# Sharing the last pair's store out in seven DMAs instead of one: two per-batch 128 x 128 maps with residuals, on one core

## The chip, the cores and the metric

One core of a Trainium2 chip runs the kernel. The metric is the device time of one execution in microseconds; lower is better. The kernel before was run three times: 644.12, 644.40 and 645.06 us, median 644.4. A fourth execution was taken with the hardware profiler and took 643.72 us.

## The reference

`x` is 128 batches of a 128 x 2048 float32 matrix. Each batch `b` has two condition numbers, which pick a 128 x 128 matrix out of 16 and out of 32, and a bias row out of 32:

```python
def _L0_cond_ref(x, weights, condition):
    W = weights[condition]
    return jnp.einsum('bct,bcd->bdt', x, W)

def _L1_cond_ref(x, subjects, weights, biases):
    w = weights[subjects]
    b = biases[subjects]
    out = jnp.einsum('bct,bcd->bdt', x, w)
    return out + jnp.transpose(b, (0, 2, 1))

x = x + _L0_cond_ref(x, L0_cond_weights, itok_B_0_15)
x = x + _L1_cond_ref(x, itok_B_0_31, L1_cond_weights, L1_cond_biases)
```

In float32, 134 MB of `x` come in and 134 MB go out.

## The kernel before

**The arithmetic.** Both steps are linear in `x`, so for one batch the result is one 128 x 128 matrix times the batch, plus a bias column: the product of (first matrix + identity) and (second matrix + identity). POOL adds the identities (lines 137 and 138), TensorE multiplies the two (`combine`, line 155), ACT copies the product out of PSUM (`copy_maps`, line 243).

**The tiling.** Two batches make a pair, and 64 pairs are worked off in order. A pair is one tile of `xt`, 128 partitions by 16 KB: partitions 0 to 63 hold the even batch, 64 to 127 the odd one, and a partition holds two neighbouring rows of a batch (2 x 2048 floats), which are contiguous in memory. `xt` has 8 slots. A pair's 32 matmuls (`pair` and `term`, line 160) go in two halves of 1024 columns into `acc0` (even batch) and `acc1` (odd batch). DVE evicts `acc0` with the bias added (`even_out`, lines 222 and 224), ACT evicts `acc1` (`odd_out`, line 247), both back into the slot that the input came from.

**The order.** There is no scheduler; each engine's instructions are written out, and semaphores link them.
- SP loads the two sets of matrices and then the pairs, one DMA of 128 partitions by 16 KB each (line 111). From the ninth pair on it waits until the slot's earlier pair has been stored.
- ACT evicts, waits for DVE's half and its own (lines 260 and 261), and issues the pair's store (line 262), again one DMA of 128 partitions by 16 KB. It goes straight on to the next pair.
- After the last pair, ACT waits for the stores of all eight slots (line 264). That is the end of its program.

Before the pairs, ACT also issues three small loads (lines 235 to 237): `cond_sb`, the condition numbers on one partition (1 x 1 KB); `bias_sb`, 128 partitions by 128 B; `cond_rep`, 32 partitions by 512 B.

A DMA that SP or ACT issues is cut into packets, one for each partition here, and the packets are shared among the core's 16 DMA engines. Each engine used writes a completion of a few bytes after its data packets; the semaphore counts up to 16. In the profile q1 is SP's queue (loads) and q10 is ACT's (stores and the three small loads).

The lines at the end of the program:

```python
                act.dma_start(out_pairs[q, :, :], xt[:, q % SLOTS, :]).then_inc(stored[q % SLOTS], LOAD)
            for q in range(SLOTS):
                act.wait_ge(stored[q], LOAD * TURNS)
```

Of the kernel before, what the change touches and what calls it, by code (L numbers as in the profile page):

```python
# [5 lines left out]
def conditioned_residual_kernel(  # L6
# [16 lines left out]
    B, C, T = x.shape  # L23
# [4 lines left out]
    SLOTS = 8  # L28
    PAIRS = B // 2
    TURNS = PAIRS // SLOTS  # L30
    LOAD = 16

    x_pairs = x.rearrange("(q k) (i u) t -> q (k i) (u t)", k=2, u=2)
    out_pairs = out.rearrange("(q k) (i u) t -> q (k i) (u t)", k=2, u=2)

    ctx = ExitStack()
    with ctx:  # L39
        def sb(name, shape, dt=fp32):  # L40
            return ctx.enter_context(nc.sbuf_tensor(name, shape, dt))
# [4 lines left out]
        def sem(name):  # L46
            return ctx.enter_context(nc.semaphore(name))
# [15 lines left out]
        xt = sb("xt", [C, SLOTS, 2 * T])  # L63
# [29 lines left out]
        hi_out1 = sem("hi_out1")  # L93
        x_loaded = [sem(f"x_loaded{q}") for q in range(SLOTS)]
        stored = [sem(f"stored{q}") for q in range(SLOTS)]

        w0T_v = w0T_sb[:, :, :].rearrange("p s (i u) -> p s u i", u=2)
        w1_v = w1_sb[:, :, :].rearrange("p s (i u) -> p s u i", u=2)
# [4 lines left out]
        @block.sync  # L103
        def _(sp):
            sp.dma_start(w0T_sb[:, :, :], w0T).then_inc(w0_loaded, LOAD)
            sp.dma_start(w1_sb[:, :, :], w1).then_inc(w1_loaded, LOAD)
            for q in range(PAIRS):
                slot = q % SLOTS
                if q >= SLOTS:
                    sp.wait_ge(stored[slot], LOAD * (q // SLOTS))  # L110
                sp.dma_start(xt[:, slot, :], x_pairs[q, :, :]).then_inc(x_loaded[slot], LOAD)

        @block.gpsimd
        def _(pool):
            nc.gpsimd.memset(ident[:, :], 0.0).then_inc(zeroed, 1)  # L115
            nc.gpsimd.iota(row[:, :], [[0, B]], base=0, channel_multiplier=1).then_inc(row_ready, 1)  # L116
            pool.wait_ge(zeroed, 1)
            nc.gpsimd.affine_select(out=ident[:, :], in_=ident[:, :], compare_op=ALU.not_equal, fill=1.0, base=0,  # L118
                                    pattern=[[-1, C]], channel_multiplier=1).then_inc(ident_ready, 1)
            pool.wait_ge(ident_ready, 1)  # L120
            pool.wait_ge(cond_loaded, LOAD)
            pool.wait_ge(w0_loaded, LOAD)
            pool.wait_ge(w1_loaded, LOAD)
            GROUP = 16
            for b in range(B):
                if b % GROUP == 0:
                    _, i0 = nc.values_load_multi_w_load_instructions(  # L127
                        cond_sb[0:1, 0, b:b + GROUP], engines=[POOL], min_val=0, max_val=S0 - 1,
                        skip_runtime_bounds_check_because="conditions index the maps")
                    _, i1 = nc.values_load_multi_w_load_instructions(  # L130
                        cond_sb[0:1, 1, b:b + GROUP], engines=[POOL], min_val=0, max_val=S1 - 1,
                        skip_runtime_bounds_check_because="conditions index the maps")
                q, k = b // 2, b % 2
                if q >= 2 and k == 0:

                    pool.wait_ge(combined, q - 1)
                nc.gpsimd.tensor_tensor(map0T[:, q % 2, k, :, :], w0T_v[:, bass.ds(i0[b % GROUP], 1), :, :], ident_v, ALU.add)  # L137
                nc.gpsimd.tensor_tensor(map1[:, q % 2, k, :, :], w1_v[:, bass.ds(i1[b % GROUP], 1), :, :], ident_v,  # L138
                                        ALU.add).then_inc(maps_ready, 1)
# [93 lines left out]
        @block.scalar  # L233
        def _(act):
            act.dma_start(cond_sb[:, :, :], conds).then_inc(cond_loaded, LOAD)
            act.dma_start(bias_sb[:, :], bias1).then_inc(bias_loaded, LOAD)
            act.dma_start(cond_rep[:, :], conds[0:1, 1, :].to_broadcast([S1, B])).then_inc(rep_loaded, LOAD)
            act.wait_ge(bias_ready, 1)

            def copy_maps(q):  # L240

                act.wait_ge(combined, q + 1)
                nc.scalar.activation(both[:, q % 2, :, :], acc1[:, CB:CB + 2 * C], ACT.Identity).then_inc(both_ready, 1)  # L243

            def odd_out(q, v, a):

                return nc.scalar.activation(xt[HC:C, q % SLOTS, v * T + a:v * T + a + HALF], acc1[v * HC:(v + 1) * HC, a:a + HALF],  # L247
                                            ACT.Identity, bias=bias_of[v * HC:(v + 1) * HC, 2 * q + 1:2 * q + 2])

            copy_maps(0)  # L250
            for q in range(PAIRS):
                act.wait_ge(lo_done1, q + 1)
                odd_out(q, 0, 0)
                if q < PAIRS - 1:
                    copy_maps(q + 1)
                odd_out(q, 1, 0).then_inc(lo_out1, 1)
                act.wait_ge(hi_done1, q + 1)
                odd_out(q, 0, HALF)
                odd_out(q, 1, HALF).then_inc(hi_out1, 1)
                act.wait_ge(hi_out0, q + 1)  # L260
                act.wait_ge(hi_out1, q + 1)
                act.dma_start(out_pairs[q, :, :], xt[:, q % SLOTS, :]).then_inc(stored[q % SLOTS], LOAD)
            for q in range(SLOTS):
                act.wait_ge(stored[q], LOAD * TURNS)


# [25 lines left out]
```

## Time and profile before

| | |
|---|---|
| three runs | 644.12, 644.40, 645.06 us |
| the profiled execution | 643.72 us, its span 641.6 us |
| DMA | 271.82 MB in 18931 packets, mean 424 GB/s over the span |
| PE busy | 525.4 us (82%) |
| DVE, ACT, POOL busy | 329.2, 309.4, 124.1 us |
| first to last store issued | 30.6 to 627.1 us |

The span runs from the first to the last instruction of the profiled execution; 2.1 us of the execution's time lie outside it. Busy shares are averages over stages with different limits. The DMA share of a window is the busy time of all packets that start in it over 16 engines' time; one engine that works alone shows as 0.06. A packet counts in the window in which it starts. Landing is the time from an issue until the last engine's completion.

### The profile page before, as it was taken

The page shows a single profiled execution, that of the slowest core. Times are in us where ns is not written, and L with a number is a line of the kernel's source. Part 1 is how long each engine was busy: PE and PEld are TensorE (multiplying, and loading weights), DVE is VectorE, ACT ScalarE, POOL GpSimd, SP SyncE. Part 2 cuts the span into 40 slices and gives each one's busy share as a digit, 9 for nine tenths or more (in the row PEclk, how much of TensorE's full clock was granted, in tenths as well). Part 3 has the DMA queues.
Part 4 walks back from the last instruction along what each step waited for, and adds up shares of the span by engine and source line. Part 5 has one row for each costly group of instructions (what it writes and reads, how often), then busy time and mean ns, then how long its engine had stood idle before and what let it go on. Part 6 is the DMA issues. An engine that isn't in the chain of part 4 may idle for free.

```text
span 641.6 us, 6679 instructions
## 1 busy us (share of the span) xinstructions
PE 525.4 (82%) x2564; PEld 224.2 (35%) x2564; DVE 329.2 (51%) x259; ACT 309.4 (48%) x321; POOL 124.1 (19%) x263
## 2 busy tenths in 40 slices
PE   1899999887787787887888977889878888779880
PEld 0344443333333333333333433333333333334330
DVE  0366666455545544554546445455554545455450
ACT  0466665444544544544446445355454445454450
POOL 2222222121221221221212212122112122121000
PEclk9999999899999999999989899899999889998896
DMA  8999999999999999999999999999999999999995
GB/s 361 436 396 434 429 430 431 428 433 430 429 431 432 433 431 430 430 430 434 429 431 431 430 433 431 430 432 430 431 431 431 432 431 429 431 431 431 430 430 246
DMA packets 18931, 271.82 MB, mean 424 GB/s; under 512 B 2241, under 2 KB 2274, under 8 KB 2274
## 3 DMA queue, kind: packets, MB, share of 16 engines
q1 hardware_dynamic: 9504, 137.37, 50.3%
q10 hardware_dynamic: 9410, 134.26, 48.9%
q8 instruction: 7, 0.11, 0.1%
q14 instruction: 10, 0.08, 0.0%
HBM read 137.40 MB, written 134.22 MB: 423 GB/s over the span
## 4 chain that ended last, share of the span: by engine, by line
DMA 75%; PE 19%; DVE 3%; ACT 1%; POOLq 0%; issue 0%; DVEq 0%; POOL 0%; SPq 0%; ACTq 0%
DMA out_dram<-xt 40%; DMA xt<-in_x_dram 33%; PE acc L160 17%; PE acc L155 1%; DMA w_sb<-in_w_dram 1%; DVE xt L222 1%; DVE xt L224 1%; ACT xt L247 0%; DVEq L39 0%; ACT L243 0%; POOLq L127 0%; POOLq L130 0%; POOL map0T L137 0%; POOL map L138 0%; ACT both L243 0%
## 5 line engine op out<-in xcount | busy, mean ns | idle before, releaser
L160 PE MATMUL acc<-xt,both 64*128 64x512 f32 x2048 | 489.8, 621 | 85.2 <-DMA xt<-in_x_dram 83.2
L247 ACT ACTIVATE xt<-acc,bias_of 64x1024 f32<-64x1024 f32 x256 | 283.6, 1108 | 300.2 <-PE acc L160 297.8
L160 PEld LDWEIGHTS acc<-xt,both 64*128 64x128 f32 x2048 | 196.2, 193 | 336.7 <-issue 223.5
L222 DVE TENSOR_SCALAR xt<-acc,bias_of 64x1024 f32<-64x1024 f32 x128 | 163.3, 1276 | 282.1 <-PE acc L160 282.1
L224 DVE TENSOR_SCALAR xt<-acc,bias_of 64x1024 f32<-64x1024 f32 x128 | 165.1, 1290 | 1.9
L137 POOL TENSOR_TENSOR map0T<-w0T_sb,ident 128x128 f32<-128x128 f32 x128 | 65.6, 512 | 469.6 <-PE acc L155 457.8
L138 POOL TENSOR_TENSOR map<-w_sb,ident 128x128 f32<-128x128 f32 x128 | 65.7, 513 | 0.0
L155 PEld LDWEIGHTS acc<-map,map0T 128*64 128x64 f32 x512 | 27.4, 137 | 49.3 <-issue 48.1
L155 PE MATMUL acc<-map,map0T 128*64 128x128 f32 x512 | 43.0, 287 | 0.9 <-POOL map L138 0.9
L243 ACT ACTIVATE both<-acc 128x256 f32<-128x256 f32 x64 | 24.5, 383 | 0.8
L146 PE MATMUL acc<-ident,bias_sb 128*32 128x128 f32 x2 | 0.6, 422 | 10.7 <-DMA bias_sb<-in_bias_dram 10.7
L243 ACT ACT_TABLE_LOAD x1 | 1.3, 1283 | 16.4 <-PE acc L155 16.4
L213 DVE TENSOR_TENSOR onehot<-cond_rep,row 32x128 f32<-32x128 int32 x1 | 0.3, 280 | 12.9 <-DMA cond_rep<-in_conds_dram 12.9
L146 PEld LDWEIGHTS acc<-ident,bias_sb 128*32 128x32 f32 x2 | 0.2, 142 | 10.7 <-DMA bias_sb<-in_bias_dram 10.7
L149 PE MATMUL acc<-onehot,biasT 32*128 32x128 f32 x2 | 0.8, 480 | 2.2 <-DVE biasT L215 2.2
L149 PEld LDWEIGHTS acc<-onehot,biasT 32*128 32x128 f32 x2 | 0.5, 304 | 2.6 <-DVE onehot L213 2.6
L217 DVE COPY bias_of<-acc 128x128 f32<-128x128 f32 x1 | 0.3, 291 | 0.9 <-PE acc L149 0.9
L215 DVE COPY biasT<-acc 32x128 f32<-32x128 f32 x1 | 0.3, 279 | 0.0
L118 POOL TENSOR_SCALAR_AFFINE_SELECT ident<-ident 128x128 f32<-128x128 f32 x1 | 0.3, 282 | 0.0
L115 POOL MEMSET ident<- 128x128 f32 x1 | 0.2, 204 | 0.3 <-POOLq L281 0.3
L116 POOL IOTA row<- 32x128 int32 x1 | 0.2, 224 | 0.0
L281 POOL MEMSET const-float32-0.0<- 128x1 f32 x1 | 0.1, 98 | 0.2 <-issue 0.2
(3 smaller groups left out, 0.3 us busy)
## 6 DMA issues: line engine op xcount, KB each, us to landing
xt<-in_x_dram SPq DMA_DIRECT2D x64, 2048.0 KB, 30.7
out_dram<-xt ACTq DMA_DIRECT2D x64, 2048.0 KB, 37.2
w_sb<-in_w_dram SPq DMA_DIRECT2D x1, 2048.0 KB, 9.4
w0T_sb<-in_w0T_dram SPq DMA_DIRECT2D x1, 1024.0 KB, 4.8
cond_sb<-in_conds_dram ACTq DMA_DIRECT2D x1, 1.0 KB
bias_sb<-in_bias_dram ACTq DMA_DIRECT2D x1, 16.0 KB, 9.4
cond_rep<-in_conds_dram ACTq DMA_DIRECT2D x1, 16.0 KB, 11.1
```

The costliest lines, as they stand in the source:

```text
L118: nc.gpsimd.affine_select(out=ident[:, :], in_=ident[:, :], compare_op=ALU.not_equal, fill=1.0, base=0, pattern=[[-1, C]], channel_multipl ...
L137: nc.gpsimd.tensor_tensor(map0T[:, q % 2, k, :, :], w0T_v[:, bass.ds(i0[b % GROUP], 1), :, :], ident_v, ALU.add)
L138: nc.gpsimd.tensor_tensor(map1[:, q % 2, k, :, :], w1_v[:, bass.ds(i1[b % GROUP], 1), :, :], ident_v, ALU.add).then_inc(maps_ready, 1)
L146: nc.tensor.matmul(acc0[0:S1, 0:C], bias_sb[:, :], ident[:, :], start=True, stop=True).then_inc(turned, 1)
L149: nc.tensor.matmul(acc1[:, 0:B], biasT[:, :, :], onehot[:, :], start=True, stop=True).then_inc(picked, 1)
L155: last = nc.tensor.matmul(acc1[k * HC:(k + 1) * HC, CB + u * C:CB + (u + 1) * C], map0T[:, buf, k, u, :], map1[:, buf, k, :, :], start=Tru ...
L160: return nc.tensor.matmul(acc[:, j * CHUNK:(j + 1) * CHUNK], both[k * HC:(k + 1) * HC, buf, u, :], xt[k * HC:(k + 1) * HC, slot, u * T + j ...
L213: nc.vector.tensor_tensor(onehot[:, :], cond_rep[:, :], row[:, :], ALU.is_equal).then_inc(onehot_ready, 1)
L222: nc.vector.tensor_scalar(xt[0:HC, q % SLOTS, a:a + HALF], acc0[0:HC, a:a + HALF], bias_of[0:HC, 2 * q:2 * q + 1], None, ALU.add)
L224: return nc.vector.tensor_scalar(xt[0:HC, q % SLOTS, T + a:T + a + HALF], acc0[HC:C, a:a + HALF], bias_of[HC:C, 2 * q:2 * q + 1], None, AL ...
L243: nc.scalar.activation(both[:, q % 2, :, :], acc1[:, CB:CB + 2 * C], ACT.Identity).then_inc(both_ready, 1)
L247: return nc.scalar.activation(xt[HC:C, q % SLOTS, v * T + a:v * T + a + HALF], acc1[v * HC:(v + 1) * HC, a:a + HALF], ACT.Identity, bias=b ...
```

## The change

`EVEN` is 2304 of the 4096 floats that a partition of the tile holds (9 KB of 16 KB). For the last pair alone, ACT issues a store of columns 0 to 2303 on all 128 partitions, and then six stores of the remaining 1792 columns (7 KB), which take 28, 35, 1, 28, 35 and 1 partitions in turn. Each of the six has its own semaphore, and ACT waits for them after the waits for the slots. Nothing else differs; the other 63 stores and all loads are the same.

```diff
+    EVEN = 2304
+    TAIL = [(0, 28), (28, 63), (63, 64), (64, 92), (92, 127), (127, 128)]
...
+        tail_stored = [sem(f"tail_stored{g}") for g in range(6)]
...
                 act.wait_ge(hi_out0, q + 1)
                 act.wait_ge(hi_out1, q + 1)
-                act.dma_start(out_pairs[q, :, :], xt[:, q % SLOTS, :]).then_inc(stored[q % SLOTS], LOAD)
+                if q < PAIRS - 1:
+                    act.dma_start(out_pairs[q, :, :], xt[:, q % SLOTS, :]).then_inc(stored[q % SLOTS], LOAD)
+            act.dma_start(out_pairs[PAIRS - 1, :, 0:EVEN], xt[:, SLOTS - 1, 0:EVEN]).then_inc(stored[SLOTS - 1], LOAD)
+            for g, (lo, hi) in enumerate(TAIL):
+                act.dma_start(out_pairs[PAIRS - 1, lo:hi, EVEN:2 * T],
+                              xt[lo:hi, SLOTS - 1, EVEN:2 * T]).then_inc(tail_stored[g], LOAD)
             for q in range(SLOTS):
                 act.wait_ge(stored[q], LOAD * TURNS)
+            for g in range(6):
+                act.wait_ge(tail_stored[g], LOAD)
```

The end of ACT's program, with its issues of DMAs, before (a row is an instruction, its line, what it writes and reads, partitions x elements):

```order
L247 ACTIVATE xt<-acc,bias_of 64x1024 x3
L262 DMA out_dram<-xt 128x4096
L247 ACTIVATE xt<-acc,bias_of 64x1024 x4
L262 DMA out_dram<-xt 128x4096
L39 UNCONDITIONAL_BRANCH
```

and after the change:

```order
L251 ACTIVATE xt<-acc,bias_of 64x1024 x3
L267 DMA out_dram<-xt 128x4096
L251 ACTIVATE xt<-acc,bias_of 64x1024 x4
L268 DMA out_dram<-xt 128x2304
L270 DMA out_dram<-xt 28x1792
L270 DMA out_dram<-xt 35x1792
L270 DMA out_dram<-xt 1x1792
L270 DMA out_dram<-xt 28x1792
L270 DMA out_dram<-xt 35x1792
L270 DMA out_dram<-xt 1x1792
L42 UNCONDITIONAL_BRANCH
```

One issue has become seven, at the same place: behind the last evictions and ahead of the final waits. No instruction of another engine moved.

## Rows read from the trace of the kernel before

**Rows 1.** Page: the span, and part 2, 40 equal slices (DMA: busy tenths of 16 engines)

```profile
span 641.6 us, 6679 instructions
...
DMA  8999999999999999999999999999999999999995
GB/s 361 436 396 434 429 430 431 428 433 430 429 431 432 433 431 430 430 430 434 429 431 431 430 433 431 430 432 430 431 431 431 432 431 429 431 431 431 430 430 246
```

**Rows 2.** Page, part 4: the chain that ended last, by engine

```profile
DMA 75%; PE 19%; DVE 3%; ACT 1%; POOLq 0%; issue 0%; DVEq 0%; POOL 0%; SPq 0%; ACTq 0%
```

**Rows 3.** Waits of SP's DMA queue: total us, times, longest

```profile
SPq L111 <- DMA out_dram<-xt: 561.2, 56, 40.1
```

**Rows 4.** Timeline from 624 us: start us, us, engine line, operation [idle before]

```profile
624.49 1.28 DVE L222 TENSOR_SCALAR xt<-acc,bias_of 64x1024 f32<-64x1024 f32 x1 [0.85 <-PE acc L160]
...
625.78 1.29 DVE L224 TENSOR_SCALAR xt<-acc,bias_of 64x1024 f32<-64x1024 f32 x1
627.10 0.34 ACTq L262 DMA_DIRECT2D out_dram<-xt  x1
```

**Rows 5.** Line 262's stores from 618 us on: issue and landing

```profile
L262 ACTq DMA_DIRECT2D out_dram<-xt x2: 338/338/338, 618.0 to 627.1; - x2
...
DMA to landing us min/median/max: 14.0/16.2/18.3
```

**Rows 6.** Windows of the tail; the last two columns are DMA share and GB/s

```profile
core 0: us, PE busy (x) PEld busy (x) DVE busy (x) ACT busy (x) POOL busy (x), PEclk, DMA share, GB/s
...
632.00:634.00 2.00, 0.00 (x0) 0.00 (x0) 0.00 (x0) 0.00 (x0) 0.00 (x0) 0.50 0.96 410
634.00:636.00 2.00, 0.00 (x0) 0.00 (x0) 0.00 (x0) 0.00 (x0) 0.00 (x0) 0.50 0.31 131
636.00:638.00 2.00, 0.00 (x0) 0.00 (x0) 0.00 (x0) 0.00 (x0) 0.00 (x0) 0.50 0.06 25
638.00:640.00 2.00, 0.00 (x0) 0.00 (x0) 0.00 (x0) 0.00 (x0) 0.00 (x0) 0.50 0.06 25
```

**Rows 7.** DMA packets that start in 632 to 636.1 us

```profile
DMA packets 82, 1.08 MB, mean 264 GB/s; under 512 B 16, under 2 KB 16, under 8 KB 16
...
q10 hardware_dynamic: 82, 1.08, 61.7%
```

**Rows 8.** DMA packets that start in 636.2 to 640 us

```profile
DMA packets 6, 0.10 MB, mean 26 GB/s; under 512 B 0, under 2 KB 0, under 8 KB 0
...
q10 hardware_dynamic: 6, 0.10, 6.0%
```

**Rows 9.** DMA packets in 612.6 to 617 us (q1 loads, q10 stores)

```profile
q10 hardware_dynamic: 127, 1.82, 96.7%
q1 hardware_dynamic: 4, 0.05, 2.7%
```

**Rows 10.** Page, part 3: all packets of the store queue

```profile
q10 hardware_dynamic: 9410, 134.26, 48.9%
```

**Rows 11.** DMA packets in 1.6 to 1.74 us, the one-partition load

```profile
DMA packets 2, 0.00 MB, mean 7 GB/s; under 512 B 1, under 2 KB 2, under 8 KB 2
...
q10 hardware_dynamic: 2, 0.00, 2.4%
```

**Rows 12.** DMA packets in 3.4 to 3.9 us, 8 KB each

```profile
DMA packets 28, 0.23 MB, mean 459 GB/s; under 512 B 0, under 2 KB 0, under 8 KB 0
...
q1 hardware_dynamic: 28, 0.23, 109.8%
```

**Rows 13.** Timeline of ACT from 0 to 6 us: its three first DMAs

```profile
0.75 0.52 ACTq L235 DMA_DIRECT2D cond_sb<-in_conds_dram  x1
1.30 0.36 ACTq L236 DMA_DIRECT2D bias_sb<-in_bias_dram  x1
1.70 0.44 ACTq L237 DMA_DIRECT2D cond_rep<-in_conds_dram  x1
```

**Rows 14.** DMA packets that start in 627.1 to 630 us

```profile
q10 hardware_dynamic: 85, 1.28, 102.9%
```

## The prediction

> **What bounds the kernel now.** I read the page first, then the last 25 us of the trace. The page shows the DMA rings busy at 0.9 of their time from the second slice to the last but one, at about 430 GB/s, and half of that in the last slice [rows 1]; the chain that ended last is three quarters DMA [rows 2], and the loads wait for stores to free their slots [rows 3]. So for 600 us the time is bytes over rate, and the change touches none of it: loads, products, evictions and the first 63 stores are the same instructions in the same order. What can change is what follows the last eviction. The timeline ends with it: the last DVE eviction starts at 625.78 and the store of pair 63 is issued at 627.10 [rows 4]. That store lands 14.0 us later, at 641.1, and the store before it needed 18.3 us [rows 5]; the span ends at 641.6.
>
> What fills these 14.0 us? The rings are full to 634; in 634:636 they are at 0.31, and from there to 641 at 0.06 and 25 GB/s [rows 6]. One busy engine of sixteen is 0.0625. So a single DMA engine works alone for the last 5 us. The packets say the same: from 632 to 636.1 sixteen completions land (packets under 512 B) [rows 7], fifteen of this store and one of the store before, which landed only at 618.0 + 18.3 = 636.3, on the late engine; from 636.2 to 640 no completion lands, and six 16 KB packets begin one after another, taking 6.0% of 16 engines' 3.8 us, that is 3.65 us or **0.608 us each** [rows 8]. The late engine starts the last store when the others have finished it: 8 packets x 0.608 = 4.9 us, from about 636.2 to 641.1. It isn't an accident of the last store. While the last load lands, from 612.6 to 617.0, the load queue shows only 4 packets, 0.05 MB [rows 9], where sixteen engines, half of whose packets are loads, would start 4.4 / 0.608 / 2 x 16 = 58: fifteen engines had finished their part, one had not. It carries a lag of 5 us into the tail, and the end of the kernel is that lag.
>
> **The change, part by part.** The store of 128 x 16 KB becomes one of 128 x 9 KB, issued first, and six small ones with 7 KB of each partition. Which engines serve the small ones decides.
>
> *How a store is shared out.* The store queue has 9410 packets [rows 10]. 64 stores x (128 data + 16 completions) = 9216; the bias load of 128 partitions adds 144; the load of the 32 partitions of condition numbers adds 48 only if it too runs on 16 engines, two partitions each; that of one partition adds 2, data and completion, and stands alone as such [rows 11]. Sum 9410, exactly. So each engine in use gets the same whole number of partitions: 8 of 128, 2 of 32, 1 of 1. I carry this over to the new shapes, which no row shows: 28 has 14 as its largest even split up to 16 (2 partitions each), 35 has 7 (5 each), 1 has 1. If the engines are always taken from the same end, the 7 KB packets fall as follows: one engine 2x(2+5+1) = 16 packets, six engines 14, seven engines 4, and **two engines none**.
>
> The Trainium skill, "DMA: Bandwidth & Descriptors", section on why a DMA increments its semaphore by 16, gives the same rule (largest k up to 16 that divides the partitions) and adds that the lowest-numbered k engines are used; that page's table of latencies says that engines 7 and 15 are usually the slow ones. By it engine 15 would get none of the 7 KB packets and engine 7 four. The rows agree as far as the shares of 128, 32 and 1 go; they don't number the engines.
>
> *The late engine's work.* An 8 KB packet takes 109.8% of 16 x 0.5 us over 28 packets [rows 12], 0.314 us, against 0.608 for 16 KB: nearly in proportion, with some 0.01 fixed. So 9 KB is 0.34 to 0.35 and 7 KB 0.27. If the late engine is one of the two left out, its last store is 8 x 0.345 = 2.76 instead of 4.86 us: **-2.1 us**. It ends at 639.0 instead of 641.1.
>
> *The other engines.* The last of the fifteen ends by 636.0 [rows 7]. In the worst case that one is also the most loaded: 2.76 + 16 x 0.27 = 7.1 against 4.86, so +2.2, 638.2. That is still 0.8 us before the late engine; the six with 14 packets stand at +1.7. Costed at nothing, with this 0.8 us as the cover.
>
> *Issues.* At the start ACT issues its three small DMAs at 0.75, 1.30 and 1.70 [rows 13], 0.4 to 0.55 us apart; the first one's packet starts within 1.0 us of its issue [rows 11]. Seven issues from 627.10 are thus out by 630.4 at the latest, and the last small store is ready at 631.4. The rings are full of earlier work and the 9 KB packets until then [rows 14], and the heavy engines come to their own sixth small store last of all. Nothing is queued on ACT behind them but the final waits. Cost nothing; without that cover, up to 0.5 us on engines that have 0.8 to spare.
>
> *Six more waits.* They stand behind the wait for the 9 KB store, which on this forecast lands last. Between the last landing (641.1) and the end of the span (641.6) there is 0.5 us, in which ACT passes its own remaining waits and the engines meet. Six more can cost from 0 to about as much again; I take 0.2, since they are all met by then.
>
> Sum: -2.1 + 0.2 = **-1.9 us**. The profiled execution took 643.7 (span 641.6 and 2.1 around it), 0.7 under the median 644.4 and 0.4 under the lowest run. From the median: 642.5.
>
> **The rivals.**
>
> *B. The late engine is in the middle group of seven.* It gets 8 x 0.345 + 4 x 0.27 = 3.84, saves 1.0, and with the waits the kernel ends 0.8 lower: 643.6. For it: seven of sixteen engines are in this group. Against it: nothing in the rows.
>
> *C, on the other side: the late engine is among the seven that carry most.* Then the change gives its longest queue to the engine that is already last: 2.76 + 14 x 0.27 = 6.54 or, with 16, 7.1: +1.7 to +2.2, and 0.2 for waits: 646.3 to 646.8. It decides from the point where the late engine's small packets exceed (4.86 - 2.76)/0.27 = 7.8, eight of them.
>
> *D. The small stores run slower than their bytes.* The heavy engines have 639.0 - (636.0 - 4.86 + 2.76) = 5.1 us for 16 packets, 0.32 each where I put 0.27; above that they end last, and at 0.45 the gain is gone. At twice the price, 0.54, they end at 642.5: +1.4 and the waits, 646.0. The rows show nothing of the kind, since in them all engines work on different parts of 128 partitions; I put its middle at no change, 644.4. The Trainium skill, "SBUF — State Buffer", port swizzle, bears on this: 28 neighbouring partitions sit behind 7 of 16 ports, so fourteen engines would read through seven. By it the 28-partition packets would take up to 0.54 and the heavy engines end near 639.3, a gain of 1.6 instead of 1.9; no run here shows it yet.
>
> *E. The shares aren't as I read them.* If 28 and 35 partitions are spread over all sixteen engines as 1 or 2 and 2 or 3, the late engine keeps 6 to 8 small packets and gains 0.5 at most: 644.1 to 644.6. If they fall on one engine each, 126 packets x 0.27 = 34 us in one queue: about 674.
>
> **How the numbers follow.** No row numbers the engines. By count the late one would be among the two left out in 2 of 16 cases, in the middle group in 7, in the heavy group in 7. I depart from that, and it is the weakest step of the forecast: the lag is so steady a trait of one engine that I take it for a place at an end of the row, and I choose the end that is left out. That is judgement and not a reading. Forecast (A) 0.56, B 0.20, C 0.11, D 0.06, E 0.07 (0.05 even, 0.02 on one engine). About 0.2% (1.3 us) is what a measurement of this kernel can tell from no change. Faster by over that, under 643.1: A, and a little of D and B: 0.59. Within it: most of B, half of D, the even part of E: 0.25. Slower: C, the rest of D and E: 0.16. Range: low end 641.8, the full 2.1 and half the scatter of the runs shown (644.12 to 645.06) below; high end 644.7, which takes in B, E and D's middle and leaves out C and the ends of D and E. A's own range is 641.8 to 643.1.
>
> **What would show each step.** In the profile after: the issue of the 9 KB store near 627 and its landing 12 us later instead of 14; the 0.06 stretch shorter by 2 us and starting about 2 us later, with packets of 9 KB in it; the other engines done by 638.2. Packets of the store queue: 9410 + 128 + 44 completions = 9582 (14 + 7 + 1 twice); another sum means other shares, E. The small stores of 28 and 35 landing by 638.5: D if later. A stretch at 0.06 with 7 KB packets that reaches beyond 641 is C. All before 627 should be as it is; if the lag before the last store isn't near 5 us, every number above moves with it.

## The result: 0.24% slower, where 0.3% faster was forecast

Over 21 runs of each, the changed kernel takes 645.86 us (644.86 to 647.23) against 644.31 us (643.3 to 646.41). The ratio is 1.0024, with a 95% interval of 1.0018 to 1.0030: slower by 1.2 to 1.9 us. The forecast was 642.5, with a range of 641.8 to 644.7. The measured time is above the range, and the sign fell on rival C's side.

### The profile after

The profiled execution took 645.86 us, its span is 644.1. First the page: the span and the 40 slices.

```profile
span 644.1 us, 6688 instructions
...
DMA  8999999999999999999999999999999999999994
GB/s 359 434 411 428 432 428 431 429 431 428 433 427 433 428 434 429 432 427 433 428 433 428 434 427 434 427 432 429 432 429 433 429 432 429 431 429 430 430 430 178
```

As in [rows 1], everything is full up to the last slice, which now moves 178 GB/s on average where it moved 246. The timeline of ACT's issues at the end (start us, us):

```profile
627.14 0.34 ACTq L268 DMA_DIRECT2D out_dram<-xt  x1
627.51 4.78 ACTq L270 DMA_DIRECT2D out_dram<-xt  x6
```

The last store is issued at 627.14, where [rows 4] has 627.10: nothing before it was changed. The seven issues take until 632.3, where the forecast had 630.4 at the latest: each of the six small ones takes 0.3 to 1.1 us, where it had 0.4 to 0.55. The windows of the tail (last columns: DMA share, GB/s):

```profile
634.00:636.00 2.00, 0.00 (x0) 0.00 (x0) 0.00 (x0) 0.00 (x0) 0.00 (x0) 0.50 0.46 190
636.00:638.00 2.00, 0.00 (x0) 0.00 (x0) 0.00 (x0) 0.00 (x0) 0.00 (x0) 0.50 0.14 59
638.00:640.00 2.00, 0.00 (x0) 0.00 (x0) 0.00 (x0) 0.00 (x0) 0.00 (x0) 0.50 0.06 25
640.00:642.00 2.00, 0.00 (x0) 0.00 (x0) 0.00 (x0) 0.00 (x0) 0.00 (x0) 0.50 0.07 29
642.00:644.00 2.00, 0.00 (x0) 0.00 (x0) 0.00 (x0) 0.00 (x0) 0.00 (x0) 0.50 0.03 11
```

[Rows 6] showed one engine alone from 636 to about 641; here it is alone from 637.3 to 643.1. So the lone engine is still there, and it works longer. What it works on is told by the packets that start from 639.25 on:

```profile
DMA packets 19, 0.10 MB, mean 26 GB/s; under 512 B 5, under 2 KB 5, under 8 KB 19
...
q10 hardware_dynamic: 19, 0.10, 6.3%
```

The landing of the 9 KB store, by its line:

```profile
DMA to landing us min/median/max: 12.6/12.6/12.6
```

The 9 KB store lands at 627.14 + 12.6 = 639.8. Of the 19 packets, 5 are completions (under 512 B): one is that of the 9 KB store, four belong to small stores. The other 14 carry 0.10 MB, 7 KB each, at a share of 6.3%, one engine. So **the late engine has 14 of the small packets**: it is one of the six of the heavy group, 2 + 5 for the first 28 and 35 partitions and 2 + 5 for the second. The page's count of the store queue is the forecast 9582, so the shares are as they were read:

```profile
q10 hardware_dynamic: 9582, 134.26, 48.8%
```

The late engine's last store is 8 x 0.344 + 14 x 0.269 = 6.5 us where it was 4.9: +1.7. That is as much as the result, and a little more.

### The profile page after: what moved, and what is told of

Read it like the earlier page. It is cut to its first block, busy times and chain, and to the rows that moved or that the text cites. A ratio compares the mean times of both kernels' runs of the same rounds, so it can differ in the third digit from the quotient of the medians.

```text
span 644.1 us, 6688 instructions
## 1 busy us (share of the span) xinstructions
PE 526.0 (82%) x2564; PEld 224.7 (35%) x2564; DVE 329.2 (51%) x259; ACT 309.4 (48%) x321; POOL 124.1 (19%) x263
## 3 DMA queue, kind: packets, MB, share of 16 engines
q10 hardware_dynamic: 9582, 134.26, 48.8%
## 4 chain that ended last, share of the span: by engine, by line
DMA 74%; PE 19%; DVE 3%; ACT 1%; POOLq 0%; issue 0%; DVEq 0%; POOL 0%; SPq 0%; ACTq 0%
DMA out_dram<-xt 40%; DMA xt<-in_x_dram 32%; PE acc L164 18%; PE acc L159 1%; DMA w_sb<-in_w_dram 1%; DVE xt L226 1%; DVE xt L228 1%; ACT xt L251 0%; DVEq L42 0%; ACT L247 0%; POOLq L131 0%; POOLq L134 0%; POOL map0T L141 0%; POOL map L142 0%; ACT both L247 0%
## 6 DMA issues: line engine op xcount, KB each, us to landing
out_dram<-xt ACTq DMA_DIRECT2D x1, 1152.0 KB, 12.6
```

## The experiments

The kernels differ from the change only in `EVEN` (the columns of the DMA of 128 partitions) and `TAIL` (the partitions of the small ones), unless a diff says more; the semaphores follow. A place is an engine's number in the order in which small DMAs take engines, counted from 0 at the end that is always taken. Load is the time that the late engine's own packets of the last store need. The kernel before was timed beside them; its medians there were 644.18, 644.24, 644.28 and 644.21.

### Where the late engine stands: a count

```diff
-    TAIL = [(0, 28), (28, 63), (63, 64), (64, 92), (92, 127), (127, 128)]
+    TAIL = [(0, 96), (96, 103), (103, 109), (109, 114), (114, 118), (118, 122), (122, 125), (125, 127), (127, 128)]
```

> The 7 KB of each partition go out in nine DMAs of 96, 7, 6, 5, 4, 4, 3, 2 and 1 partitions. By the reading of the shares (largest even split, always from the same end) these run on 16, 7, 6, 5, 4, 4, 3, 2 and 1 engines, with 6 partitions for each engine of the first and one for each of the others. Theory H (the late engine is one of the first seven places, since it worked off 14 small packets after the change): it takes 6 packets and then one more for each DMA whose count of engines reaches its place, so the completions that it writes alone at the end number its place: 7 more for place 1, 6 for 2, 5 for 3, 3 for 4, 2 for 5, 1 for 6 (places from 0). Its work in the last store is 2.76 + (6 + N) x 0.27, so between 4.7 and 6.3 us against 4.86 before. Theory P (the late engine is slow because of what it is given here, not by place): it takes 6 packets and none or all of the rest, or another engine ends last. Store queue: 9410 + 224 - 128 + 48 + 16 packets = 9216 + 192 + 2 + 128 + 48 = 9586 by the reading of the shares.

One execution: 645.39 us. The page counts 9586 packets in the store queue, as expected. The last packets of all, those that start from 641.56 on:

```profile
DMA packets 7, 0.02 MB, mean 26 GB/s; under 512 B 4, under 2 KB 4, under 8 KB 7
...
q10 hardware_dynamic: 7, 0.02, 6.3%
```

Seven packets one after another, 4 of them completions: that of the 96-partition DMA, and then three small packets with a completion each. Three small DMAs reach the late engine, those of 7, 6 and 5 partitions, and none of those of 4 or fewer. Its place is 4, the fifth. Theory P falls.

### The same bytes, seven DMAs, even shares

```diff
-    TAIL = [(0, 28), (28, 63), (63, 64), (64, 92), (92, 127), (127, 128)]
+    TAIL = [(0, 16), (16, 48), (48, 64), (64, 80), (80, 112), (112, 128)]
```

> The same bytes in the same number of DMAs (9 KB of 128 partitions, then six), but the six take 16, 32, 16, 16, 32 and 16 partitions, so that each runs on 16 engines and each engine again has 8 partitions. Theory H (the loss comes from 14 small packets on the late engine where 8 were): nearly all of the loss is gone; what is left is the price of splitting, 8 x (0.345 + 0.27 - 0.608) = 0.06 us on the late engine, six completions on it and up to 0.2 us of waits: 0 to +0.4 us against the kernel before. Theory S (splitting itself costs: seven issues that took 0.3 to 1.1 us each and six more waits): the loss stays at about +1.5 us.

645.46 us, ratio 1.0018 (1.0009 to 1.0027): +0.6 to +1.7 us. This is neither theory. The load of the late engine says +0.1; the loss is most of the change's. The late engine's packets around the border between the 9 KB store and the first small one:

```profile
DMA packets 1, 0.01 MB, mean 5 GB/s; under 512 B 0, under 2 KB 0, under 8 KB 0
...
q10 hardware_dynamic: 1, 0.01, 6.2%
```

The same view from that packet's end to the last completion:

```profile
DMA packets 15, 0.06 MB, mean 25 GB/s; under 512 B 7, under 2 KB 7, under 8 KB 15
...
q10 hardware_dynamic: 15, 0.06, 6.2%
```

In the first window, 1.68 us long, a single 9 KB packet starts and fills 6.2%, the whole time of one engine: it took 1.67 us, where its seven predecessors took 0.35 each. Behind it, 8 data packets and 7 completions pass at the normal pace. So a packet at a border between DMAs can be stretched, here by 1.3 us, with all other engines done. That is a new cost, and it became theory B.

The late engine isn't the only one that meets it. The packets that start from 635.25 to 636, while the others work on their last small packets:

```profile
DMA packets 21, 0.12 MB, mean 165 GB/s; under 512 B 5, under 2 KB 5, under 8 KB 20
...
q10 hardware_dynamic: 21, 0.12, 93.8%
```

93.8% of 16 x 0.75 us is 11.3 us. Without one 16 KB packet and five completions, 10.6 us are left for 15 packets of 7 KB, 0.71 us each in place of 0.27. In this trace 26 of the 128 packets of 7 KB took over 0.32 us; in the change's first profile it is 3 of 128.

### Fourteen places

```diff
-    TAIL = [(0, 28), (28, 63), (63, 64), (64, 92), (92, 127), (127, 128)]
+    TAIL = [(0, 126), (126, 128)]
```

> The 7 KB go in two DMAs, of 126 partitions (14 engines with 9 each by the reading of the shares) and of 2. Theory H: the late engine is one of the first fourteen and gets 9 small packets, or 10 if it is one of the first two: 2.76 + 9 x 0.27 = 5.2 us against 4.86, so +0.3 to +0.7 us against the kernel before. Theory S: two more DMAs in place of six, a third of +1.5 us, +0.5 us; this run doesn't tell H from S alone but shows with e2 whether both are needed. If the late engine were one of the last two it would be -2 us.

644.92 us, ratio 1.0014 (1.0004 to 1.0023), +0.3 to +1.5. The profile shows 9 data packets and 2 completions of the late engine behind the 9 KB store:

```profile
DMA packets 11, 0.06 MB, mean 26 GB/s; under 512 B 2, under 2 KB 2, under 8 KB 11
...
q10 hardware_dynamic: 11, 0.06, 6.3%
```

As the even split of 126 says: 14 engines with 9. The load gives +0.3, at the low end of the interval, and the last 9 KB packet was stretched by 0.3 us.

### Twice the bytes in the uneven part

```diff
-    EVEN = 2304
+    EVEN = 512
```

> The same six groups of 28, 35, 1, 28, 35 and 1 partitions, but 14 KB of each partition in them and 2 KB in the DMA of 128. Issues and waits are as in the change. Theory H: the late engine has 8 x 0.08 + 14 x 0.53 = 8.1 us against 4.86, +3.2 us and 0.2 for the waits, +3.4 against the kernel before, twice what the change costs. Theory S: the same +1.5 us as the change, since the instructions are the same.

647.80 us in four runs, ratio 1.0059 (1.0044 to 1.0074), +2.8 to +4.8: theory H's +3.4, with the change's own instructions. The loss follows the bytes that the late engine is given. Theory S, with +1.5, lies outside the interval.

### One split only

```diff
-    TAIL = [(0, 28), (28, 63), (63, 64), (64, 92), (92, 127), (127, 128)]
+    TAIL = [(0, 128)]
```

> The last store is cut once: 9 KB and 7 KB of all 128 partitions, both on 16 engines, so the late engine keeps 8 packets of each. Theory L (load alone): one more DMA costs the 7 ns in which two packets exceed one, 8 times, a completion and a wait: 0.1 to 0.2 us over the kernel before. Theory B (each border between DMAs in the late engine's row of packets can stretch a packet by 0.3 to 1.3 us, as it did in the profiles of the counts, the even split and the fourteen places): one border, 0.2 to 0.7 us on average. A loss of over 1 us would say that splitting as such is the cost.

644.49 us, ratio 1.0003 (0.9994 to 1.0012). One cut costs nothing that can be measured. No packet of the late engine's was stretched in its profile.

### Places 0 to 3 alone take the rest

```diff
-    EVEN = 2304
-    TAIL = [(0, 28), (28, 63), (63, 64), (64, 92), (92, 127), (127, 128)]
+    EVEN = 3072
+    TAIL = [(0, 124), (124, 128)]
```

> The count showed that the late engine writes three completions behind the 96-partition DMA, those of 7, 6 and 5 partitions: its place is 4, the fifth. Here 12 KB of each partition go in a DMA of 128 and 4 KB in DMAs of 124 and of 4 partitions, which by the reading of the shares run on 4 engines (31 partitions each, then 1), places 0 to 3, so that the late engine gets none. Theory H (the late engine's own load sets the end): it has 8 x 0.455 = 3.6 us instead of 4.86, -1.2 us; the four others end at about 636.0 - 4.86 + 3.64 + 32 x 0.155 = 639.7, just under its 639.9; with up to 0.5 us for two borders -0.5 to -1.2 us against the kernel before. If the late engine's place isn't 4 but below, it gets 32 packets of 4 KB more: +3.7 us.

643.68 us, ratio **0.9988** (0.9979 to 0.9997): faster than the kernel before, by 0.2 to 1.4 us. The windows of the tail:

```profile
634.00:636.00 2.00, 0.00 (x0) 0.00 (x0) 0.00 (x0) 0.00 (x0) 0.00 (x0) 0.50 0.31 125
636.00:638.00 2.00, 0.00 (x0) 0.00 (x0) 0.00 (x0) 0.00 (x0) 0.00 (x0) 0.50 0.30 121
638.00:640.00 2.00, 0.00 (x0) 0.00 (x0) 0.00 (x0) 0.00 (x0) 0.00 (x0) 0.50 0.19 80
640.00:642.00 2.00, 0.00 (x0) 0.00 (x0) 0.00 (x0) 0.00 (x0) 0.00 (x0) 0.50 0.00 0
```

The lone stretch at 0.06 is gone. 0.30 is five engines of sixteen, four on 4 KB packets and the late one on 12 KB packets; nothing starts after 640. The same cut as in the change, aimed at places that leave the late engine out, turns the sign.

### One partition more: five places

```diff
-    EVEN = 2304
-    TAIL = [(0, 28), (28, 63), (63, 64), (64, 92), (92, 127), (127, 128)]
+    EVEN = 3072
+    TAIL = [(0, 125), (125, 128)]
```

> As the kernel with four places (12 KB in a DMA of 128, 4 KB in two small ones), but the small ones take 125 and 3 partitions instead of 124 and 4. By the reading of the shares 125 runs on 5 engines, places 0 to 4, with 25 partitions each. Theory H with place 4: the late engine now gets 25 packets of 4 KB, 8 x 0.457 + 25 x 0.156 = 7.6 us against 4.86, +2.7 us against the kernel before, where 124 partitions gave -0.8. If the late engine's place were 5 or above, this kernel would be faster than with 124, by about -1.2 us; if it were below 4, the one with 124 could not have been faster than the kernel before.

648.22 us, ratio 1.0065 (1.0048 to 1.0082), +3.1 to +5.3. Against 124 partitions, one more partition costs 4.5 us (648.22 - 643.68; the two were timed on different chips, beside kernels before of 644.21 and 644.24). The packets from the late engine's last border on, and the one before it:

```profile
DMA packets 27, 0.10 MB, mean 25 GB/s; under 512 B 2, under 2 KB 2, under 8 KB 27
...
q10 hardware_dynamic: 27, 0.10, 6.3%
```

The same view of the stretch just before:

```profile
DMA packets 1, 0.01 MB, mean 8 GB/s; under 512 B 0, under 2 KB 0, under 8 KB 0
...
q10 hardware_dynamic: 1, 0.01, 6.2%
```

The 27 packets are 25 of 4 KB and two completions, on one engine, which with 124 partitions has none of the 4 KB packets; and again one packet at the border that fills its 1.5 us alone, where its neighbours took 0.46. Load (+2.7) and one stretch (+1.1) make 3.8, inside the interval. The place is 4: 125 partitions hit it, 124 miss it.

### POOL issues the small stores

```diff
-    EVEN = 2304
-    TAIL = [(0, 28), (28, 63), (63, 64), (64, 92), (92, 127), (127, 128)]
+    EVEN = 1024
+    TAIL = [(0, 5), (5, 126), (126, 128)]
...
+            pool.wait_ge(hi_out0, PAIRS)
+            pool.wait_ge(hi_out1, PAIRS)
+            for g, (lo, hi) in enumerate(TAIL):
+                pool.dma_start(out_pairs[PAIRS - 1, lo:hi, EVEN:2 * T],
+                              xt[lo:hi, SLOTS - 1, EVEN:2 * T]).then_inc(tail_stored[g], LOAD)
+            for g in range(3):
+                pool.wait_ge(tail_stored[g], LOAD)
...
-            for g, (lo, hi) in enumerate(TAIL):
-                act.dma_start(out_pairs[PAIRS - 1, lo:hi, EVEN:2 * T],
-                              xt[lo:hi, SLOTS - 1, EVEN:2 * T]).then_inc(tail_stored[g], LOAD)
...
-            for g in range(6):
-                act.wait_ge(tail_stored[g], LOAD)
```

> 4 KB of each partition in a DMA of 128 by ACT, the other 12 KB in three DMAs that POOL issues, of 5, 121 and 2 partitions. If POOL's DMAs use as many engines as the largest even split, and each begins where the one before stopped, they run on places 0 to 4, 5 to 15 and then 0 and 1, so that the late engine (place 4) has 8 packets of 4 KB and one of 12 KB, 1.7 us instead of 4.86, and ends near 638.0; the eleven others have 8 x 0.155 + 11 x 0.455 = 6.2 us, +1.4, and end near 637.4. Theory H: -3 us against the kernel before, less up to 1 us for POOL's start. If POOL spreads each DMA over all engines, the late engine keeps 8 packets of 12 KB: 0 to +0.7 us. If they run from the lowest place each time, the late engine has 11 or 1.

645.12 us, ratio 1.0018 (1.0008 to 1.0028). A miss: the hoped for 3 us did not come. The packets of both queues from 637.9 on, when one engine is left:

```profile
DMA packets 20, 0.13 MB, mean 24 GB/s; under 512 B 5, under 2 KB 5, under 8 KB 13
...
q10 hardware_dynamic: 13, 0.08, 3.5%
q0 software_dynamic: 7, 0.05, 2.1%
```

The last engine still alternates between 12 KB packets of POOL's queue (q0) and 16 KB packets of the store before, and then does the 4 KB ones. POOL's DMA of 121 partitions did not pass it by, so there was no relief. The seven packets of q0 with 0.05 MB hold four of 12 KB, where the reading "each begins where the one before stopped" gave this engine one in all: that reading falls. Followed back packet by packet, the late engine has at least eight of them, as an even spread over all engines would give. For that the expectation said 0 to +0.7 us; the interval is +0.5 to +1.8, and in this profile two of the engine's 16 KB packets took 0.90 and 1.11 us in place of 0.61. On which engines each of POOL's three DMAs ran wasn't settled.

### Small packets again, in two DMAs

```diff
-    TAIL = [(0, 28), (28, 63), (63, 64), (64, 92), (92, 127), (127, 128)]
+    TAIL = [(0, 63), (63, 128)]
```

> The 7 KB go in two DMAs instead of six, of 63 partitions (7 engines with 9 each by the reading of the shares) and of 65 (13 engines with 5 each). The late engine, place 4, again has 14 small packets, as in the change, but with two borders in its row instead of five, and with four issues and waits fewer. Theory H (its load alone): 2.78 + 14 x 0.269 - 4.86 = +1.7 us against the kernel before, the same as the change. Theory S (the even split in six cost +1.1 to +1.3 where its load says +0.1, so a good part of the change's +1.55 is splitting): +0.6 to +1.0 us.

645.90 us, ratio 1.0029 (1.0016 to 1.0041), +1.0 to +2.6. The expectation had a slip: the largest even split of 63 up to 16 is 9 engines with 7 partitions, not 7 with 9. The profile shows what that makes of the late engine, 12 data packets, 7 and 5, and 3 completions, one of them the 9 KB store's:

```profile
DMA packets 15, 0.09 MB, mean 22 GB/s; under 512 B 3, under 2 KB 3, under 8 KB 15
...
q10 hardware_dynamic: 15, 0.09, 6.3%
```

The same view of one packet in the middle of these:

```profile
DMA packets 1, 0.01 MB, mean 7 GB/s; under 512 B 0, under 2 KB 0, under 8 KB 1
...
q10 hardware_dynamic: 1, 0.01, 6.3%
```

Load: 2.76 + 12 x 0.269 - 4.86 = +1.1. The second window shows one 7 KB packet that takes 0.96 us in place of 0.27, and the last 9 KB packet was stretched by 0.28: together +2.1. So two small DMAs can cost as much as the change's six. That the number of DMAs costs nothing isn't shown by it: in this kernel two packets were stretched, and at equal load six even DMAs lost 1.2 us.

Its even twin:

```diff
-    TAIL = [(0, 28), (28, 63), (63, 64), (64, 92), (92, 127), (127, 128)]
+    TAIL = [(0, 64), (64, 128)]
```

> The 7 KB go in two DMAs of 64 partitions, 16 engines with 4 each, so the late engine keeps 8. Theory H: +0.1 us (two more completions, 8 x 7 ns). Theory S (a price of some 0.2 us for each DMA, from the even split in six): +0.4 us, between the one split (+0.2) and the six (+1.2).

644.36 us, ratio 1.0006 (0.9995 to 1.0016): nothing that can be measured, as the load says (+0.1); +0.4 isn't excluded.

### Second profiles of the two kernels

> The kernel before, unchanged, for a second profile: how late the late engine is before the last store (5.1 us in the first profile, 5.2 to 6.3 in those of the changed kernels) and whether any packet of its last store is stretched. Theory L: the lag differs from one execution to the next, 5 to 6.3 us also here, and explains the differences between profiles but not the difference of medians. Theory B: no packet of the last store over 0.65 us, since it has no border inside.

> The change itself, unchanged, for a second profile. Theory H: the late engine again writes 8 packets of 9 KB and 14 of 7 KB last, in 6.5 us when none is stretched. Theory B: a packet at one of its borders is stretched by 0.3 us or more, as in three of the other split kernels.

One execution each: 644.46 and 646.35 us. The DMA packets in the second profile of the kernel before, while the late engine is alone:

```profile
DMA packets 10, 0.13 MB, mean 26 GB/s; under 512 B 2, under 2 KB 2, under 8 KB 2
...
q10 hardware_dynamic: 10, 0.13, 6.2%
```

The same view of the change, behind the 9 KB store:

```profile
DMA packets 18, 0.10 MB, mean 26 GB/s; under 512 B 4, under 2 KB 4, under 8 KB 18
...
q10 hardware_dynamic: 18, 0.10, 6.3%
```

Before: 8 packets and a completion (the first completion is that of the store ahead), 4.9 us, none stretched. The change: 14 small packets and four completions in 3.8 us, none stretched. So in both profiles of the change the late engine's own row is all load: 6.5 against 4.9 us. What differs from one execution to the next is when it begins. The landing of the last store but one, issued at 618.27 in the second profile of before, at 618.06 and 617.94 in the two of the change:

```profile
DMA to landing us min/median/max: 18.3/18.3/18.3
```

The same of the change, first profile:

```profile
DMA to landing us min/median/max: 19.0/19.0/19.0
```

And of the change, second profile:

```profile
DMA to landing us min/median/max: 19.6/19.6/19.6
```

It lands at 636.6 before (and at 636.3 in the first profile), at 637.1 and 637.5 with the change. In the profiles of the other kernels with all stores on ACT's queue it lies between 636.3 and 637.6, though their code up to there is the same. So the late engine's start scatters by about 1 us, and a comparison of two profiles contains it: of the 2.5 us between the spans 641.6 and 644.1, 0.7 is that start and 1.7 is the load. Medians of many runs average out what is scatter. That all of it is scatter isn't shown: both profiles of the kernel before lie at the low end. One thing goes with it. The change's first profile has, from 621.5 to 622.5,

```profile
q8 instruction: 1, 0.02, 5.8%
```

a fetch of 16 KB of instructions. The seven profiles with such a fetch between 620 and 624 us have this landing at 637.0 to 637.6, the six without it (two of them the kernel before's) at 636.3, 636.3, 636.4, 636.4, 636.6 and 637.2. Whether the fetch delays the late engine, and whether the change makes it come there, was not tested.

### The account

Load is the late engine's last store by its packets (0.344 for 9 KB, 0.269 for 7 KB, 0.457 for 12 KB, 0.532 for 14 KB, 0.156 for 4 KB, 0.080 for 2 KB, read from starts that follow one another) less 4.86, or, for the 124 partitions, the end of the four others as far as the expectation could bound it.

| kernel | small DMAs | late engine's small packets | load says, us | measured, us (95%) |
|---|---|---|---|---|
| the change | 6 | 14 | +1.7 | +1.5 (+1.2 to +1.9) |
| 14 KB uneven | 6 | 14 of 14 KB | +3.2 | +3.8 (+2.8 to +4.8) |
| 125 and 3 | 2 | 25 of 4 KB | +2.7 | +4.2 (+3.1 to +5.3) |
| 63 and 65 | 2 | 12 | +1.1 | +1.9 (+1.0 to +2.6) |
| 126 and 2 | 2 | 9 | +0.3 | +0.9 (+0.3 to +1.5) |
| even split in six | 6 | 8 | +0.1 | +1.2 (+0.6 to +1.7) |
| 64 and 64 | 2 | 8 | +0.1 | +0.4 (-0.3 to +1.0) |
| one split | 1 | 8 | +0.1 | +0.2 (-0.4 to +0.8) |
| 124 and 4 | 2 | 0 | -0.5 to -1.2 | -0.8 (-1.4 to -0.2) |

The load tells the losses of over 3 us and the gain from the rest, but it doesn't order the small losses: the even split in six has no extra load and by its median loses nearly what the change does, and their intervals overlap. That the change's own +1.5 us is load therefore rests on its two profiles, in which nothing on the late engine was stretched, and on the kernel with 14 KB, which has the same instructions; it doesn't follow from the medians of these two.

## Why the prediction was wrong

**What held.** The bound of the kernel: the lag of one DMA engine, which works alone for 5 us (the last store's packets run from 635.8 to 640.7 in the trace, not from 636.2 to 641.1, since a landing is noted 0.4 to 0.5 us after the last packet; the 4.9 us are the same). The shares, from the packet count of [rows 10]: 28 on 14 engines, 35 on 7, 1 on 1, confirmed to the packet by 9582, and by 9586, by 9 for 126, 25 for 125. The prices of packets: 0.344 and 0.269 us against 0.345 and 0.27. That the others end in time: by 637.3, where 638.2 was the bound. Rival D falls: from 634.3 to 636.3, while the heavy engines work on their small packets,

```profile
DMA packets 56, 0.34 MB, mean 172 GB/s; under 512 B 12, under 2 KB 12, under 8 KB 53
...
q10 hardware_dynamic: 56, 0.34, 40.9%
```

56 packets take 40.9% of 32 us, 13.1 us. With 41 of 7 KB at 0.272, 3 of 16 KB at 0.611 and 12 completions at 0.009 the sum is 13.1 as well: no slowing by neighbouring partitions there. In the whole tail 125 of the 128 packets of 7 KB took 0.272 us, the other three 0.46 to 0.61. By the prediction's estimate from the Trainium skill ("SBUF — State Buffer", port swizzle) the 28-partition packets would have taken up to 0.54; the trace doesn't show it.

**Small misses without effect.** The issues were out by 632.3, not 630.4; the late engine was on its 9 KB packets until 639.3. Under rival E the late engine would keep 6 to 10 small packets, not 6 to 8.

**The step that failed** is the one the prediction called its weakest: "I take it for a place at an end of the row, and I choose the end that is left out", with 0.56. The late engine's place is 4, in the group with 14 packets. The rows gave no number, the count alone gave 7 of 16 to that group against 2 of 16 to the group that was chosen, and the forecast set the count aside for a guess. With the count's chances, C had to get 7/16 of the 0.87 that A, B and C share, 0.38, and "slower" 0.43 and not 0.16. The Trainium skill, "DMA: Bandwidth & Descriptors", latency table, says that engines 7 and 15 are usually the slow ones. Its best guess at the cause concerns DMAs issued by GpSimd, and this kernel has none. By the prediction's reading these two would have had four small packets or none, and the measured late engine has 14. If that page is right that the lowest-numbered engines are taken first (section on why a DMA increments its semaphore by 16), then the slow one here is engine 4, by the count and by 124 against 125 partitions; no run numbers the engines.

**The size, by rival C's own sum.** C said +1.7 and 0.2 for six more waits, 1.9; measured were 1.5 (1.2 to 1.9). The waits cost 0.1 us at most: from the last packet's end to the end of the span it is 0.9 us in both profiles of the kernel before and 1.0 in both of the change.

**What was missing.** "Costed at nothing" for the cut itself. The even split in six costs 0.6 to 1.7 us with no load to explain it, and in the profiles of eight of the nine other kernels that split on ACT's queue (all but the one split) some packet of the late engine's took 0.05 to 1.3 us more than its size, some of them the last of a DMA and about as many inside one, so the border isn't shown to be what matters. In the two profiles of the change it met none. Whether these stretches are the excess in the account, and what makes them, was not settled: in the even split the stretched packet came 4 us after the last small store had been issued, so a late issue doesn't explain it, and the scatter of the lag is of the same size.

**What the traces show of the lag itself.** In the trace of the kernel before, 13,776 of the 14,445 packets of 16 KB that start from 60 to 610 us took 0.611 us. 602 took 0.613 to 0.66, and only 22 of these overlap the next one, so nearly all can be one engine's. Followed back from its last store, the late engine took 0.615 to 0.634 for each of its packets from 621.1 to 626.1. So it falls behind packet by packet; why its packets take longer is not shown.

## What to carry to other kernels

When a kernel ends on DMA, look at how many engines are still at work in its last microseconds: a share of 0.06 is one of sixteen, and only its queue matters. On ACT's queue a DMA's partition count set how many engines serve it and which (the largest even split up to 16, always from the same end here), so a cut can relieve or burden the late engine; find its place with a row of small DMAs of 7, 6, 5, ... partitions and count its completions before aiming a split. Where the place isn't known, give each group its chance by count.

## What the runs showed of the hardware that was not expected

One DMA engine ends 5 us behind the fifteen others, and in all the profiles in which the shares tell it, on three chips, this is consistent with one fixed place. Its 16 KB packets took up to 0.634 us where the others' took 0.611. Moving one partition from a DMA, 125 to 124, takes 25 packets off that engine and 4.5 us off the kernel. A packet ahead of a border between two DMAs on one engine took 1.67 us in place of 0.35, with all other engines idle. Issues of small DMAs behind a full queue took 0.3 to 1.1 us each on ACT in the change, where the large one took 0.34. The version with 124 and 4 partitions beats both kernels by a hair, 643.68 us against 644.24 and 645.86.
